# Edge groups of one tile instead of two in a sorted graph-attention kernel

## What is computed

```python
edge_index = stack([src, dst])            # 206250 edges: 100000 both ways, and 6250 self loops
xn = layernorm(x)                         # 6250 nodes x 256
Wh = xn @ W.T + b                         # 4 heads of 64
e = leaky_relu(alpha_src[idx_i] + alpha_dst[idx_j], 0.2)
out = segment_sum(softmax_by_idx_i(e) * Wh[idx_j], idx_i)      # graph attention
x = x + out + linear_attention_block(xn)  # "mix": qkv, kv sums, layernorm, gelu MLP
x = x + moe_ffn(layernorm(x))             # shared MLP and 4 experts, best 2 of 4
```

## Time and profile before

| | us |
|---|---|
| median of 3 runs | 3117.58 |
| the profiled execution | 3118.8 |
| its span | 3117.0 |
| stage one, by the profile | 0 to about 560 |
| lots of stage two | about 563 to 3071 |
| the last pieces alone | about 3066 to 3117 |

### The profile page before, as it was taken

One profiled execution on the slowest core, in us unless ns is written; L12 is line 12 of the kernel. 1 busy time (PEld: TensorE's weight loads), 2 busy tenths in 40 slices (PEclk: granted clock), 3 DMA queues, 4 the chain that ended last, 5 costly groups with the idle time before them and its releaser, 6 DMA issues.

```text
span 3117.0 us, 40701 instructions
## 1 busy us (share of the span) xinstructions
PE 2181.7 (70%) x10817; PEld 1529.3 (49%) x10818; DVE 1882.2 (60%) x3946; ACT 792.2 (25%) x1396; POOL 2160.0 (69%) x2141
## 2 busy tenths in 40 slices
PE   1001984177778787787977879778778787787877
PEld 0000552155555555555655556555555555555554
DVE  8998552265664656666566664656655656666463
ACT  6000442022222222222222222222222222222222
POOL 1008777677777777777777777777777777777770
PEclk6555997588989988989889898889989988989988
DMA  6000221434344444444444444444444444444462
GB/s 188 0 0 13 75 74 41 96 101 119 96 103 124 102 111 116 104 123 103 115 110 104 122 102 124 102 103 123 102 106 124 102 117 108 105 123 103 123 91 29
DMA packets 271584, 306.05 MB, mean 98 GB/s; under 512 B 164258, under 2 KB 210856, under 8 KB 271080
## 3 DMA queue, kind: packets, MB, share of 16 engines
q0 software_dynamic: 97760, 251.60, 30.9%
q1 hardware_dynamic: 140098, 18.08, 3.9%
q10 hardware_dynamic: 33480, 33.36, 3.4%
HBM read 276.25 MB, written 26.62 MB: 97 GB/s over the span
## 4 chain that ended last, share of the span: by engine, by line
PE 50%; DVE 14%; issue 8%; POOL 6%; ACT 2%; DMA 1%; ACTq 0%; DVEq 0%; POOLq 0%; SPq 0%; another core or an unknown queue 0%
PE sum_banks L1027 26%; PE f_banks L1042 9%; POOL gathered L965 6%; DVE onehot L1430 5%; PE turned L999 3%; PE f_banks L1161 2%; DVE gathered L1451 2%; PE f_banks L1086 1%; PE sum_banks L1015 1%; PE f_banks L1067 1%; PE f_banks L1162 1%; DVE he L1579 1%; DVE he L1582 1%; PE f_banks L1068 1%; ACT onehot_t L1202 1%
## 5 line engine op out<-in xcount | busy, mean ns | idle before, releaser
L965 POOL DMA_INDIRECT gathered<-table,col x1872 | 1898.4, 1014 | 572.9 <-issue 563.2
L1027 PE MATMUL sum_banks<-gathered,onehot 128*128 128x260 f32 x3744 | 1070.5, 449 | 105.7 <-DVE gathered L1451 104.4
L1027 PEld LDWEIGHTS sum_banks<-gathered,onehot 128*128 128x128 f32 x3744 | 824.8, 226 | 298.1 <-issue 133.0
L1451 DVE TENSOR_TENSOR gathered<-gathered 128x512 f32<-128x512 f32 x936 | 591.4, 692 | 50.6 <-ACT gathered L1206 47.8
L1430 DVE TENSOR_TENSOR onehot<-iota_row,col 128x1024 f32<-128x1024 f32 x236 | 288.9, 1225 | 448.4 <-PE sum_banks L1027 448.0
L290 POOL DMA_INDIRECT edge_list<-payload,pos x244 | 249.9, 1024 | 293.4 <-DVE pos L411 216.5
L1202 ACT COPY onehot_t<-turned 128x1024 bf16<-128x1024 bf16 x236 | 238.6, 1011 | 332.5 <-PE turned L999 330.2
L1216 ACT COPY acc<-sum_banks x234 | 87.8, 375 | 915.4 <-PE sum_banks L1027 700.0
L999 PE MATMUL turned<-ident_bf,onehot 128*128 128x128 bf16 x1888 | 157.7, 231 | 165.6 <-DVE onehot L1430 165.5
L999 PEld LDWEIGHTS turned<-ident_bf,onehot 128*128 128x128 bf16 x1888 | 115.3, 103 | 183.7 <-DVE onehot L1430 145.6
L1009 PE MATMUL scores<-t,onehot_t 128*128 x1880 | 100.1, 175 | 122.0 <-DVE scored L1439 82.0
(11 more groups left out here) (322 smaller groups left out, 2564.0 us busy)
## 6 DMA issues: line engine op xcount, KB each, us to landing
gathered<-table,col POOLq DMA_INDIRECT x1872
xn_batch<-xn ACTq DMA_DIRECT2D x13, 512.0 KB, 4.3
x_all<-in_x SPq DMA_DIRECT2D x1, 6144.0 KB
x_batch<-in_x ACTq DMA_DIRECT2D x12, 512.0 KB
out<-xf ACTq DMA_DIRECT2D x12, 512.0 KB
edge_list<-xn_all SPq DMA_DIRECT2D x2, 2176.0 KB, 14.1
edge_list<-payload,pos POOLq DMA_INDIRECT x244
col<-edge_list SPq DMA_DIRECT2D x236, 8.0 KB, 2.1
```

What stands on the lines that cost most here:

```text
L965: g.indirect_dma_start(gathered[:, l, t, :], None, sh["table"], bass.IndirectOffsetOnAxis(ap=col[l][:, t // G, t % G, 0:1], axis=0)).then_ ...
L1027: last = t.matmul(sum_banks[:, ds(banks_of[g], 1), 0:TB].rearrange("p a w -> p (a w)"), onehot[:, l % 3, g * G + k, :], gathered[:, l, g * ...
L1451: v.tensor_tensor(value, value, gathered[:, l, tiles, C:TB].unsqueeze(3).broadcast_to([P, G, H, HD]), ALU.mult).then_inc(s_mul, 1)
```

## The change

A group becomes one tile, a lot eight groups; a lot has 8 tiles as before. The tables have twice the groups (LOT_WORDS 10, and 8 words of `blk` a lot). The waits of TensorE on products stay one for two tiles. The two tables share columns of SBUF, `lots` on partition 0 and `blk` on partition 32, and buffers of the 13 turns of stage one lie in memory that the sort has left, with a wait for the padding's DMA ahead of the turns on VectorE and ScalarE.

```diff
-G = 2
+G = 1
 GR = G * P
-GROUPS = 4
+GROUPS = 8
+PAIRS = G * GROUPS // 2
...
-        xT = [sb("xT", [P, 2, W4]), keys[1][:, 0:2 * W4].rearrange("p (k w) -> p k w", k=2)]
-        wh = [sb("wh", [P, BATCH, C + 2 * H]),
+        late = spare[:, 0:2 * TE]
+        xT = [late[:, 0:2 * W4].rearrange("p (k w) -> p k w", k=2), keys[1][:, 0:2 * W4].rearrange("p (k w) -> p k w", k=2)]
+        wh = [late[:, 2 * W4:2 * W4 + BATCH * (C + 2 * H)].rearrange("p (b c) -> p b c", b=BATCH),
...
-        k_min = sb("k_min", [P, 2, C])
-        k_exp = sb("k_exp", [P, 2, C])
-        kk = sb("kk", [P, 2, C])
-        vv = sb("vv", [P, 2, 2, KVC])
-        y = [sb("y", [P, BATCH, C]), keys[1][:, 2 * W4:2 * W4 + BATCH * C].rearrange("p (b c) -> p b c", b=BATCH)]
+        pads = pad_rows[:, :, :].rearrange("p r w -> p (r w)")
+        k_min, k_exp, kk = (pads[:, i * 2 * C:(i + 1) * 2 * C].rearrange("p (a c) -> p a c", a=2) for i in range(3))
+        vv = pads[:, 6 * C:6 * C + 4 * KVC].rearrange("p (b a w) -> p b a w", b=2, a=2)
+        y = [late[:, 2 * TE - BATCH * C:2 * TE].rearrange("p (b c) -> p b c", b=BATCH), keys[1][:, 2 * W4:2 * W4 + BATCH * C].rearrange("p (b c) -> p b c", b=BATCH)]
...
             dve.wait_ge(s_bias_out, 1)
+            dve.wait_ge(s_filled, 32)
...
             act.wait_ge(s_bias, 1)
+            act.wait_ge(s_filled, 32)
...
                 for g in range(GROUPS):
-                    pe.wait_ge(s_mul, n * GROUPS + (g + 1))
+                    if g * G % 2 == 0:
+                        pe.wait_ge(s_mul, n * PAIRS + (g * G // 2 + 1))
                     for k in range(G):
...
-            def product(it, l, g):
-
-                tiles = slice(g * G, g * G + G)
+            def product(it, l, pair):
+
+                tiles = slice(pair * 2, pair * 2 + 2)
                 value = gathered[:, l, tiles, 0:C].rearrange("p k (a d) -> p k a d", d=HD)
-                v.tensor_tensor(value, value, gathered[:, l, tiles, C:TB].unsqueeze(3).broadcast_to([P, G, H, HD]),
+                v.tensor_tensor(value, value, gathered[:, l, tiles, C:TB].unsqueeze(3).broadcast_to([P, 2, H, HD]),
                                 ALU.mult).then_inc(s_mul, 1)
...
-                for g in range(GROUPS):
-                    product(it, l, g)
+                for pair in range(PAIRS):
+                    product(it, l, pair)
...
+        tables = sb("tables", [2 * 32, NG // GROUPS * LOT_WORDS], I32)
...
-            "blk": sb("blk", [1, NG], I32),
-            "lots": sb("lots", [1, NG // GROUPS, LOT_WORDS], I32),
+            "blk": tables[32:33, 0:NG],
+            "lots": tables[0:1, :].rearrange("a (l w) -> a l w", w=LOT_WORDS),
```

More of the change, by code:

```diff
@@ L180, in stage_sort_and_mix @@
         inv = sb("inv", [P, BATCH])
-        xT = [sb("xT", [P, 2, W4]), keys[1][:, 0:2 * W4].rearrange("p (k w) -> p k w", k=2)]
-        wh = [sb("wh", [P, BATCH, C + 2 * H]),
+        late = spare[:, 0:2 * TE]
+        xT = [late[:, 0:2 * W4].rearrange("p (k w) -> p k w", k=2), keys[1][:, 0:2 * W4].rearrange("p (k w) -> p k w", k=2)]
+        wh = [late[:, 2 * W4:2 * W4 + BATCH * (C + 2 * H)].rearrange("p (b c) -> p b c", b=BATCH),
               keys[0][:, 0:BATCH * (C + 2 * H)].rearrange("p (b c) -> p b c", b=BATCH)]
-        k_min = sb("k_min", [P, 2, C])
-        k_exp = sb("k_exp", [P, 2, C])
-        kk = sb("kk", [P, 2, C])
-        vv = sb("vv", [P, 2, 2, KVC])
-        y = [sb("y", [P, BATCH, C]), keys[1][:, 2 * W4:2 * W4 + BATCH * C].rearrange("p (b c) -> p b c", b=BATCH)]
+        pads = pad_rows[:, :, :].rearrange("p r w -> p (r w)")
+        k_min, k_exp, kk = (pads[:, i * 2 * C:(i + 1) * 2 * C].rearrange("p (a c) -> p a c", a=2) for i in range(3))
+        vv = pads[:, 6 * C:6 * C + 4 * KVC].rearrange("p (b a w) -> p b a w", b=2, a=2)
+        y = [late[:, 2 * TE - BATCH * C:2 * TE].rearrange("p (b c) -> p b c", b=BATCH), keys[1][:, 2 * W4:2 * W4 + BATCH * C].rearrange("p (b c) -> p b c", b=BATCH)]
+        assert 2 * W4 + BATCH * (C + 2 * H) + BATCH * C <= 2 * TE
         assert 2 * W4 + BATCH * C <= SLOTS and BATCH * (C + 2 * H) <= SLOTS
```

## The result

The changed kernel takes 3203.61 us (median of 4 runs, 3191.3 to 3213.12) beside 3118.43 of the kernel before (median of 4): a ratio of 1.0271, 95% interval 1.0233 to 1.0309. The forecast was 3101, its range 3073 to 3119. It is slower by 85 us where it was to be faster by 17.

What follows compares the result with a forecast made beforehand. The TensorE and VectorE chain was taken as the bound, 191.1 us per 18 lots against POOL's 189. 3118.8 - 52.4 - 4.9 - 1.3 + 36 + 5 = 3101 to 3102, median 1.2 lower: 3101; range 3073 to 3119.

Steps and rivals of the forecast that it cites:

- Fewer iterations: Whole lot loop: one-tile groups drop one plain iteration, 6 lots and 48 gathers, saving 52.4 us on the chain.
- The tail: Last lots: VectorE's wait for the late padding gathers goes, saving 4.9 us; the last sums had been 11.8 us apart.
- Stage one: Ahead of the lots: L415 and the sum behind it each take 1.2 us more, hidden by 48 us before POOL's scatter.
- The col loads: DMA queue: 1024 pieces of 8 bytes for 512 of 16, 8% of the engines at most; cost 0.
- More words in the register loads: TensorE's `lots` load, 9 words for 5: odd lots +0.93 us, even +0.26, paid in plain lots; 36 us in all.
- the sums start straight after the zeroing and take 3.77: Plain lots 1 to 5: why the longer `lots` load is paid there, 3.3 us a batch.
- The loads of `blk` and the address operations: TensorE's sequencer, 8 `blk` words for 4 and doubled address operations: mostly hidden, 0.5 us a batch, 5 in all.
- They run while the array works off 3.77 us of sums: Plain lots: `blk` loads and address operations are hidden, some 0.9 us of cover ahead of L1009.
- 0.66 us against 0.55 us of wait for the one-hot: Where VectorE's scores come last: extra `blk` load and address work against the transposes' existing wait, nearly covered.
- Rival (d): Work ahead of L1009 uncovered, `lots` load paid in 12 lots a batch: 10.5 us a batch, 3174 us, chance 0.10.
- turning point of 5.3 us a batch: Added TensorE sequencer cost per batch from which the rival of 3174 us decides, 58.6 / 11.
- marks over 196: Sign of being wrong: batch marks over 196 us apart, with L1009 starting late behind the sums in plain lots.

Runs made afterwards that it cites:

- kernel of 3092 us: Changed kernel with rows of 12 words and banks loaded before the transposes in plain lots 1 to 5, 3091.74 us, or that plus useless matmuls at seams, 3092.31.
- the two fastest: Changed kernel, rows of 12, banks loaded before plain lots' transposes, next `blk` load ahead of the second piece: 3079.71 us; with useless matmuls added: 3085.23.
- experiments 2: Changed kernel with rows of `lots` lengthened to 12 words (48 bytes, every row on 16 bytes), 9 loaded as before: 3117.86 us, ratio 1.0007.
- experiment 3: Kernel before with rows of `lots` of 8 words, every row on 16 bytes, 5 loaded as before: 3115.58 us, ratio 1.0007.
- experiment 1: Kernel before with only the longer load: rows of 10 words, 9 loaded, 5 used: 3213.3 us, ratio 1.0324.
- experiment 5: Changed kernel with two useless float32 matmuls added between transposes and banks load in odd plain lots: 3181.96 us, ratio 1.0207.
- experiment 6: Kernel before with 9 words loaded from rows of 12: 3120.56 us; the same plus all the change's `blk` loads and address operations: 3188.08 us.
- the early load: Changed kernel, rows of 12, TensorE's banks load moved between by_node and transposes: 3127.24 us in all lots, 3091.74 in plain lots 1 to 5 only.

## Why the prediction was wrong, step by step

The whole account, step by step from one kernel to the next, in us: before 3116.0; 9 words from aligned rows + 4.3 (3120.6 against 3116.3); the register work + 67.5; the iteration - 70.2 (3188.1 to the changed kernel with rows of 12, 3117.9); rows off 16 bytes + 85.7; together 3203.3. Against the forecast's terms, the loads of `lots` cost 90 for 36, the register work 67.5 for 5, and the iteration gave 70 for 59.

*Fewer iterations*: right in kind. The worked plan gave the 228 lots. Its worth was put at 52.4 + 4.9 + 1.3 = 58.6 and came out as 70.2. Of that, 42 to 44 us are the fourth iteration in the trace with all the register work (240.5 us for that batch, 196 to 199 for one of three), where its lots take mostly 6.4 to 8.2 us; most of the rest is 1.6 us in each other batch and some 6 us in the first iterations. The two kernels differ a little in how `blk` is loaded (two loads of 332 ns or one of 593), and I can't say that this is not it.

*The tail*: right, but hardly put to the test, as the chain came 100 us later than forecast, long after the gathers. The last two lots' sums start 7.87 us apart (3151.35 and 3159.22), not 11.8, and VectorE doesn't wait for the last gathers. In the kernel of 3092 us, nearest to the forecast's 3101, they are 6.62 apart; in the two fastest the wait is back (12.09 and 10.14). *Stage one*: right; the scatter ends at 560.8, the first lot's sums start at 617.0 (618.3 before). *The col loads*: their queue takes 5.7% of the DMA engines (3.9 before), under the 8 forecast; that they cost nothing was not tried by itself.

*More words in the register loads*: the duration of each load was right to 0.02 us, the gaps too, and the alignment (experiments 2 and 3 show it by changing the row's length alone). The size of the term was wrong: 36 forecast, 98 measured by itself (experiment 1). The failed step is "the sums start straight after the zeroing and take 3.77": the price of a gap was taken as its own length, with the work behind it at its old duration. A gap of 1.84 us was outside all gaps ahead of the zeroing matmul in the plain lots of before (0.95 at most), and the rows that could have warned were at hand: in the earlier trace rows the sums behind a wait of 3.33 take 5.46 us instead of 3.77. I read them as a wait for VectorE and not as a price of the wait. The lot after it in the same mix iteration of before has a pause of the very length:

```profile
1591.88 5.41 PE L1027 MATMUL sum_banks<-gathered,onehot 128*128 128x260 f32 x16 [1.84 <-DVE gathered L1451]
```

The rival in which the gap lowers the clock was missing.

The Trainium skill, "TensorE: Matmul & The Clock Gate", section "HAM oscillation — how this bites in real kernels", tells of a kernel whose waits for DMA between bursts of matmuls let the clock fall, so that each burst starts slow. Here the pause comes from a register load and not from a DMA; the trace of the changed kernel and experiment 5 agree with the rest (6.47 us and 3.77); experiment 3, with slow sums behind a gap of 0.26, isn't explained by the gap ahead of it.

*The loads of `blk` and the address operations*: 5 forecast, 67.5 measured. The step that failed is "They run while the array works off 3.77 us of sums": a cover read in a plain lot was taken for all. In plain lots it does hold (the scores follow the sums at once in the changed kernel). Where VectorE's scores come last there is no such cover, as the load stands behind the wait for them. The prediction did look there, and set 0.66 us against 0.55 us of wait for the one-hot; in experiment 6 the pause there is 1.4 us longer and the scores take 0.5 us longer, the 0.55 us are used up, and behind the longer pause the clock is at its low level. Rival (d), "TensorE's sequencer becomes the bound", with 3174 and 10%, came nearest; but it put the cost ahead of the scores of plain lots, where it doesn't lie, and in the load ahead of the sums (4 us in experiment 6), and had nothing on the clock. Its turning point of 5.3 us a batch was passed: the changed kernel with all effects stands at 203.1 - 191.2 = 11.9 a batch. The sign of being wrong that was written down, marks over 196, did come, but not from scores that start late in plain lots, which it was tied to.

The Trainium skill, "Runtime: NRT & Kernel Launch", section "Instruction fetch mechanics", has some 200 ns a register; the estimate by it was 44 for 36. Off 16 bytes 2186 / 9 = 243 ns is near it, on 16 bytes 844 / 9 = 94 is not. Neither saves the forecast.

*The sum*: adding the terms was not what failed. Measured each by itself they come to 98 + 67.5 - 70 = + 95 us, and the kernel is 85 to 87 us slower. Two of the terms were far too small, and both for having priced TensorE's idle time as its own length: it can cost twice, once itself and once in the clock.

## What to carry to other kernels

Before a change puts a longer pause ahead of TensorE's work, look in the trace for a pause of that length and read how long the work behind it takes: that, and not the old duration, is the price to expect (here 5.4 to 6.5 us behind 28 of 33 such pauses; behind the other 5 the sums stayed at 3.77). Whether an instruction's sequencer work is hidden has to be read at each kind of place, above all where it stands behind a wait that ends last; here moving a load ahead of a piece of other work gave some 10 us. Rows of a table that the sequencer loads are best laid on 16 bytes, even if padded: 9 words took 0.85 us there and 2.18 at 8 beside, worth 86 us here, though nothing for rows of 5 words (experiment 3). And when TensorE is mended, look which engine sets the pace next.

## What I had not expected of the hardware

A register load off 16 bytes costs as if it went word by word to its end: 2186 ns for 9 words and 1238 for 5, 237 for each of the four between; on 16 bytes they take 844 and 590, and 8 words 593. (One place is out of this: in the last lot of the feed-forward iteration of the changed kernel with rows of 12, the 8 words of `blk`, on 16 bytes as everywhere, take 0.99 to 1.60 us. Why is open.) The length of the pause alone doesn't set the granted clock. In the changed kernel a pause of 1.85 us left it at 1.00 (zeroing matmul at 1756.49, its 0.28 us that of the high clock, and the 16 records behind it in 3.77), and experiment 3 has a fall behind 0.26:

```profile
1756.49 0.28 PE L1019 MATMUL sum_banks<-zeros 1*128 1x260 bf16 x1 [1.85 <-issue]
1756.72 3.77 PE L1032 MATMUL sum_banks<-gathered,onehot 128*128 128x260 f32 x16
```

```profile
1662.00:1663.40 1.40, 0.86 (x10) 0.56 (x10) 1.40 (x4) 0.39 (x1) 1.09 (x2) 1.00 0.37 95
1663.40:1665.00 1.60, 1.60 (x5) 1.31 (x5) 1.57 (x4) 0.62 (x1) 1.29 (x2) 0.54 0.38 101
```

(The second fence is the windows view of the kernel before with rows of 8 words.) What decides between such places stays open; no run here settles it. It may also be why gains of a microsecond or two a batch in plain lots came through in some kernels (the early load) and not in others (rows of 8 words).
